# First attention of a four-block kernel: Q projected by halves through K's bank, K through the transposes' bank, a third tile transposed on VectorE, a score ring of 17 places

## What is computed

```python
Q = einsum('bse,hec->bhsc', X, Wq) + bq      # 16 heads, 128 columns: Q1 | Q2, 64 each
K = einsum('bse,hec->bhsc', X, Wk) + bk
V = einsum('bse,hed->bhsd', X, Wv) + bv
A1 = einsum('bhqd,bhkd->bhqk', Q1, K1) * s
A2 = einsum('bhqd,bhkd->bhqk', Q2, K2) * s
P = softmax(A1, axis=-1) - lam * softmax(A2, axis=-1)
O = einsum('bhqk,bhkd->bhqd', P, V)
Y = transpose(O).reshape(...) @ Wo + bo      # then a layer norm
```

## Time and profile before

| | |
|---|---|
| median of 3 runs | 1575.24 us (1575.03 to 1578.04) |
| the profiled execution | 1573.77 us, its span 1572.0 us |
| TensorE matmul busy | 1439.6 us, 92% |
| VectorE busy | 1376.4 us, 88% |
| ScalarE busy | 1198.3 us, 76% |
| GpSimd busy | 1003.8 us, 64% |
| chain that ended last | TensorE 53%, ScalarE 14%, VectorE 13%, issue 11%, GpSimd 7% |
| VectorE, row maxima of the first attention (line 1152) | 512 x 1216 ns = 620.1 us |
| ScalarE, exponentials (line 847) | 512 x 1116 ns = 570.6 us |
| GpSimd, subtractions (line 656) | 256 x 2360 ns = 604.2 us |

### The profile page before, as it was taken

One profiled execution on the slowest core, in us unless ns is written; L12 is line 12 of the kernel. 1 busy time (PEld: TensorE's weight loads), 2 busy tenths in 40 slices (PEclk: granted clock), 3 DMA queues, 4 the chain that ended last, 5 costly groups with the idle time before them and its releaser, 6 DMA issues.

```text
span 1572.0 us, 28031 instructions
## 1 busy us (share of the span) xinstructions
PE 1439.6 (92%) x10243; PEld 588.5 (37%) x10243; DVE 1376.4 (88%) x2107; ACT 1198.3 (76%) x1911; POOL 1003.8 (64%) x727
## 2 busy tenths in 40 slices
PE   5899999999999999999999999986685999999985
PEld 1434443344434443344334433434541222222223
DVE  6798998999899989999999989988687999999947
ACT  4787888888888888888888888874342888888882
POOL 2999998898898988989889889880032011111112
PEclk9999999999999999999999999997696999999997
DMA  4243433343244323433343333420000110000001
GB/s 126 76 105 92 106 86 82 102 112 90 78 103 110 96 77 104 109 92 85 91 107 105 83 91 93 114 68 1 1 22 21 31 35 15 16 16 16 16 16 34
DMA packets 154641, 110.80 MB, mean 70 GB/s; under 512 B 31381, under 2 KB 142906, under 8 KB 154506
## 3 DMA queue, kind: packets, MB, share of 16 engines
q1 hardware_dynamic: 154378, 108.99, 26.5%
q0 software_dynamic: 128, 0.03, 0.0%
HBM read 53.82 MB, written 34.87 MB: 56 GB/s over the span
## 4 chain that ended last, share of the span: by engine, by line
PE 53%; ACT 14%; DVE 13%; issue 11%; POOL 7%; DMA 1%; SPq 0%; POOLq 0%; ACTq 0%; DVEq 0%
PE PS L1573 14%; PE PS L1585 10%; PE PS L1599 9%; ACT ering L847 7%; PE PS L1980 4%; POOL ering L656 3%; DVE nmx L1152 2%; PE PS L1942 2%; DVE region L1172 2%; PE PS L1632 2%; PE PS L1964 2%; ACT region L871 2%; DVE mxp L1479 2%; ACT ering L1059 2%; POOL ering L655 2%
## 5 line engine op out<-in xcount | busy, mean ns | idle before, releaser
L1152 DVE TENSOR_REDUCE nmx<-PS 128x1 f32<-128x1024 f32 x512 | 620.1, 1216 | 54.4 <-PE PS L1574 53.5
L847 ACT ACTIVATE ering<-PS,nmx 128x1024 f32<-128x1024 f32 x512 | 570.6, 1116 | 109.6 <-DVE nmx L1152 109.5
L656 POOL TENSOR_TENSOR ering<-ering 128x1024 f32<-128x1024 f32 x256 | 604.2, 2360 | 21.4
L1573 PE MATMUL PS<-region 64*128 64x512 f16 x1536 | 405.1, 381 | 20.4 <-ACT ering L847 14.5
L1574 PE MATMUL PS<-region 64*128 64x512 f16 x1536 | 405.2, 381 | 0.0
L655 POOL TENSOR_SCALAR ering<-ering,rho 128x1024 f32<-128x1024 f32 x256 | 287.3, 1122 | 95.2 <-DVE rho L1161 94.5
L1479 DVE TENSOR_REDUCE mxp<-PS 128x2 f32<-128x1024 f32 x256 | 304.2, 1222 | 34.3 <-PE PS L1964 29.9
L1059 ACT ACTIVATE ering<-PS 128x1024 f32<-128x1024 f32 x256 | 259.6, 1024 | 70.0 <-PE PS L1942 64.1
L1585 PE MATMUL PS<-ident,ering 128*128 128x128 f32 x1536 | 251.5, 286 | 15.6 <-ACT t L858 8.1
L1585 PEld LDWEIGHTS PS<-ident,ering 128*128 128x128 f32 x1536 | 161.6, 141 | 201.7 <-issue 73.8
L1573 PEld LDWEIGHTS PS<-region 64*128 64x128 f16 x1536 | 112.6, 94 | 261.3 <-ACT ering L847 110.2
(11 more groups left out here) (301 smaller groups left out, 1876.2 us busy)
## 6 DMA issues: line engine op xcount, KB each, us to landing
ptd<-t SPq DMA_DIRECT2D x256, 128.0 KB, 2.4
region<-region SPq DMA_DIRECT2D x64, 256.0 KB, 3.5
t<-ptd SPq DMA_DIRECT2D x44, 256.0 KB, 3.5
region<-ptd SPq DMA_DIRECT2D x44, 256.0 KB, 3.5
va<-ptd SPq DMA_DIRECT2D x20, 256.0 KB, 3.4
acc<-ptd SPq DMA_DIRECT2D x20, 256.0 KB, 3.5
osb<-scr SPq DMA_DIRECT2D x32, 128.0 KB, 3.3
rcp<-scr SPq DMA_DIRECT2D x32, 128.0 KB, 3.3
```

Of the source, the lines that this page charges most:

```text
L656: P.tensor_tensor(e1, e1, e2, ALU.subtract).then_inc(s_sub_ok, 1)
L847: A.activation((E1, E2)[p][s % 4], PS[:, bank:bank + 2, :].rearrange("p a b -> p (a b)"), ACT.Exp, bias=nmx[:, 2 * s + p:2 * s + p + 1], s ...
L1152: V.tensor_reduce(nmx[:, 2 * s + p:2 * s + p + 1], PS[:, bank:bank + 2, :].rearrange("p a b -> p (a b)"), AX.X, ALU.max, negate=True).then ...
L1573: MM(PS[:, bank, :], top[0:64, ql, q], KT[b][0:64, p, kl, :], start=(j == 0), stop=(j == 2))
```

## The change

- `BY_DVE` becomes (0, 1, 2): tile 1 goes over VectorE too. VectorE turns tiles 0, 1, 2 in steps 3, 4, 5, with the two `stage` buffers and DRAM buffers used in turn, counted by c = 3n + i. TensorE turns tiles 3 to 7 (in steps 6, 7, 0, 1, 2).
- Q is projected in two halves of 512 columns in MISC, in steps 0 and 1, where K was; ScalarE and VectorE split each half in steps 1 and 2. Q's place in the ring goes.
- K's halves are projected into TRB, in steps 3 and 5; they are split in steps 3 and 4 (part 0) and 5 (part 1). The first transposes of tile 3 wait for K's last low half, and the first half of K waits for the last eviction of tile 7.
- The ring has 17 places a pass, so it begins on another pair in each pass, and the out-projection's pair moves with it.
- On TensorE, score p=1 stands ahead from step 3 on; the key tiles of values are dealt out as 3, 2, 2, 1; tile 3's two halves stand together behind the values of step 6.
- GpSimd's `part_w` takes Wq and Wk together, three instructions for five, and goes one tile later. SP's load of Wk for the second head moves to the end of its pass.

The diff, cut to its core:

```diff
-        wq_s = sb("wq_s", [128, 128])
-        wk_s = sb("wk_s", [128, 128])
+        wqk_s = sb("wqk_s", [128, 2, 128])
...
-        BY_DVE = (0, 2)
+        BY_DVE = (0, 1, 2)
...
-        def ring(v):
-            at = v + (1 if v >= 1 else 0) + (1 if v >= 5 else 0)
-            return 2 * (at % 3)
-        Y_PAIR, Q_PAIR = 2, 0
+        def turn_of(n, v):
+            return 17 * n + v + (1 if v >= 1 else 0)
+        def ring(n, v):
+            return 2 * (turn_of(n, v) % 3)
+        def y_pair(m):
+            return 2 * ((turn_of(m + 2, 1) - 1) % 3) if m + 2 < last0 else 2
+        def q_done(m, i):
+            return 2 * m + i if m else 1
+        def q_place(m, i):
+            if m == 0:
+                return PS[:, 0:2, :].rearrange("p a b -> p (a b)"), slice(0, T)
+            return MISC, slice(HF * i, HF * i + HF)
+        def k_place(m, part):
+            if m == 0:
+                return (MISC, PS[:, 2, :])[part]
+            return TRB
...
             def store_blocks(n, i):
-                sp.wait_ge(s_bt_ok, 2 * n + i + 1)
-                if n >= 1:
-                    sp.wait_ge(s_ptr_dma[(n - 1) % 2], 64 * ((n - 1) // 2 + 1))
+                c = len(BY_DVE) * n + i
+                sp.wait_ge(s_bt_ok, c + 1)
+                if c >= 2:
+                    sp.wait_ge(s_ptr_dma[c % 2], 32 * (c // 2))
...
-                P.tensor_copy(wqh[:, 0, :], wq_s[:, :])
-                link(P.tensor_copy(wkh[:, 0, :], wk_s[:, :]))
-                P.tensor_tensor(wqh[:, 1, :], wq_s[:, :], wqh[:, 0, :], ALU.subtract)
-                P.tensor_tensor(wkh[:, 1, :], wk_s[:, :], wkh[:, 0, :], ALU.subtract).then_inc(s_wlo_ok, 1)
+                link(P.tensor_copy(wqkh[:, :, 0, :], wqk_s[:, :, :]))
+                P.tensor_tensor(wqkh[:, :, 1, :], wqk_s[:, :, :], wqkh[:, :, 0, :], ALU.subtract).then_inc(s_wlo_ok, 1)
...
                     if s == 2 and nxt and own:
-                        high_k(n + 1, 1)
+                        high_q(n + 1, 1)
...
                     if s == 1 and nxt and own:
-                        high_k(n + 1, 0)
+                        high_q(n + 1, 0)
                     if later and (s + 5) % 8 in BY_PE:
                         keep_t(m, (s + 5) % 8, 0)
                     if own:
                         exponent(n, s, 0)
...
                     if later and (s + 5) % 8 in BY_PE:
                         keep_t(m, (s + 5) % 8, 1)
-                    if s == 2 and nxt and own:
-                        high_q(n + 1)
+                    if s == 5 and nxt and own:
+                        high_k(n + 1, 1)
                     if own:
                         exponent(n, s, 1)
+                    if s == 3 and nxt and own:
+                        high_k(n + 1, 0)
...
                         maximum(n, s, 0)
+                    if s == 4 and nxt and own:
+                        low_k(n + 1, 0)
...
                     if s == 1 and nxt and own:
-                        low_k(n + 1, 0)
+                        low_q(n + 1, 0)
                     if own if s else prv:
                         weigh(n if s else n - 1, (n if s else n - 1) % 2, (s + 7) % 8)
                     if s == 2 and nxt and own:
-                        low_k(n + 1, 1)
+                        low_q(n + 1, 1)
...
-                    if s == 2 and nxt and own:
-                        low_q(n + 1)
-                    if own and s in (3, 5):
-                        turn_blocks(n, s // 2 - 1)
+                    if own and s - 3 in BY_DVE:
+                        turn_blocks(n, BY_DVE.index(s - 3))
+                    if s == 5 and nxt and own:
+                        low_k(n + 1, 1)
...
                 if v == 3 and n >= 2:
                     pe.wait_ge(s_y_ok, n - 1)
-                elif v == 7 and n + 1 < last0:
-                    pe.wait_ge(s_qlo_ok, n + 2)
-                elif v in (1, 2, 5, 6):
+                elif v in (1, 2):
                     at_least(pe, s_exp, u - 1)
                 else:
                     at_least(pe, s_exp, u - 2)
...
                 at_least(pe, s_tr_ev, turned(n, s) + i)
+                if (s, i) == (BY_PE[0], 0) and n + 1 < last0:
+                    pe.wait_ge(s_klo_ok, 2 * (n + 2))
...
-                if m >= 1:
-                    pe.wait_ge(s_exp, 16 * (m - 1) + 3)
-                for i in range(2):
+                if m >= 1 and i == 1:
+                    pe.wait_ge(s_qlo_ok, q_done(m, 0))
+                elif m == 1:
+                    pe.wait_ge(s_klo_ok, 2)
+                    pe.wait_ge(s_xt_ev, 4)
+                elif m >= 2:
+                    pe.wait_ge(s_v_ev, m + 1)
+                    at_least(pe, s_on_ok, m - 2)
+                for k in range(2) if m == 0 else (i,):
...
-                elif part == 1:
+                dst = k_place(m, part)
+                if m >= 1 and part == 1:
                     pe.wait_ge(s_klo_ok, 2 * m + 1)
...
+                elif m >= 1:
+                    at_least(pe, s_tr_ev, turned(m - 1, 0))
...
-            PIECES = {3: (0, 1, 2), 4: (3,), 5: (4, 5, 6), 6: (7,)}
+            PIECES = {3: (0, 1, 2), 4: (3, 4), 5: (5, 6), 6: (7,)}
...
-                    if own and s >= 4:
+                    if s == 5 and nxt and own:
+                        project_k(n + 1, 1)
+                    if own and s >= 3:
                         scores(n, s, 1)
-                    if later and (s + 5) % 8 in BY_PE:
+                    if later and s != 6 and (s + 5) % 8 in BY_PE:
                         turn(m, (s + 5) % 8, 0)
-                    if s == 2 and nxt and own:
-                        project_q(n + 1)
+                    if s == 3 and nxt and own:
+                        project_k(n + 1, 0)
...
                         for j in PIECES[s]:
                             values(n - 1, j)
+                    if s == 6 and later:
+                        turn(m, 3, 0)
...
-                    if own and s < 4:
+                    if own and s < 3:
                         scores(n, s, 1)
                     if later and (s + 5) % 8 in BY_PE:
                         turn(m, (s + 5) % 8, 1)
...
                     if s in (0, 1) and nxt and own:
-                        project_k(n + 1, s)
+                        project_q(n + 1, s)
```

More of the change, by code:

```diff
@@ L147, in two_layers @@
         iota = xs[:, :, :].rearrange("p l t -> p (l t)").bitcast(F32)
-        wqh, wkh = [r16(15360 + 256 * i, 256).rearrange("p (l c) -> p l c", l=2) for i in range(2)]
+        wqkh = r16(15360, 512).rearrange("p (i l c) -> p i l c", i=2, l=2)
+        wqh, wkh = wqkh[:, 0, :, :], wqkh[:, 1, :, :]
         G2 = eflat[:, 4096:8192].rearrange("p (k n) -> p k n", n=N)
@@ L504, in _ @@
                         sp.dma_start(wo_s[64 * k:64 * k + 64, :], a["L0_attn_Wo"][h * D0:h * D0 + D0, :]).then_inc(s_ld_wo, 16)
[L505 to L509, removed]
+                if own and b == 0 and 0 < h < H0 - 1:
+                    sp.wait_ge(s_wlo_ok, h)
                     sp.dma_start(wk_s[:, :], a["L0_attn_Wk"][h + 1]).then_inc(s_ld_wk, 16)
@@ L525, in _ @@
                     load_turned(n, 0)
-                    store_blocks(n, 1)
-                    load_turned(n, 1)
+                    for i in range(1, len(BY_DVE)):
+                        store_blocks(n, i)
+                        load_turned(n, i)
+                if n == 0:
+                    sp.wait_ge(s_k0_mm, 4)
+                    sp.dma_start(wk_s[:, :], a["L0_attn_Wk"][1]).then_inc(s_ld_wk, 16)
             sp.wait_ge(s_wprep_ev, 3)
@@ L838, in exponent @@
                 u = 16 * n + 2 * s + p
-                bank = ring(2 * s + p)
+                bank = ring(n, 2 * s + p)
                 act.wait_ge(s_max, u + 1)
@@ L843, in exponent @@
                     if tile in BY_DVE:
-                        act.wait_ge(s_bt_ok, 2 * prev + BY_DVE.index(tile) + 1)
+                        at_least(act, s_bt_ok, len(BY_DVE) * prev + BY_DVE.index(tile) + 1 if prev >= 0 else 0)
                     else:
@@ L1552, in scores @@
                 u = 16 * n + v
-                bank = ring(v)
+                bank = ring(n, v)
                 if v == 0:
                     pe.wait_ge(s_klo_ok, 2 * (n + 1))
-                    pe.wait_ge(s_qlo_ok, n + 1)
+                    pe.wait_ge(s_qlo_ok, 2 * n + 1)
                     pe.wait_ge(s_qx_dma, 32 * (n + 1))
@@ L1593, in values @@
                 if j == 0:
-                    pe.wait_ge(s_ptr_dma[n % 2], 64 * (n // 2 + 1))
+                    c = len(BY_DVE) * n + len(BY_DVE) - 1
+                    for i in range(2):
+                        pe.wait_ge(s_ptr_dma[i], 32 * ((c - i) // 2 + 1))
                 if j % 4 == 0:
@@ L1612, in to_out, with project_q @@
                     r = slice(64 * half, 64 * half + 64)
-                    mm = MM(PS[:, Y_PAIR + half, :], wo_s[r, :], on[r, :], start=True, stop=True)
```

(3 more changed lines are left out.)

82 lines of the change are left out of this document (38 added, 44 removed).

## The result

| | before | changed |
|---|---|---|
| median | 1575.03 us (7 runs, 1572.80 to 1578.04) | 1582.37 us (7 runs, 1580.47 to 1588.75) |
| span of the profiled execution | 1572.0 us | 1578.7 us |
| VectorE busy | 1376.4 us, 88% | 1412.3 us, 89% |
| TensorE matmul busy | 1439.6 us, 92% | 1402.7 us, 89% |
| ScalarE busy | 1198.3 us, 76% | 1172.0 us, 74% |

The ratio is 1.0051, 95% interval 1.0036 to 1.0066: slower by half a per cent. The time lies inside the range (1566 to 1586), 6.4 us above the 1576.0 forecast, but outside the forecast's own range (1571 to 1580), and its sign is not that of the likeliest case, "same".

What follows compares the result with a forecast made beforehand. A closed chain of hand-overs bounds each pass: 14.06 + 3.37 + 4.44 + 4.24 + 4.86 + 0.86 = 31.83 us against 31.77. With start-up and last pass +0.3 us, 1575.5 on the median's scale, given as 1576.0; range 1566 to 1586.

Steps and rivals of the forecast that it cites:

- the likeliest case, "same": Whole kernel's time unchanged within what a measurement can tell, about 0.2%; chance 0.44, against slower 0.37 and faster 0.19.
- (a): VectorE from max 8 to max 15 (row maxima of scores 8 and 15) without a gap: 14.06 us.
- (b): From max 15 over exponential 15 and score 1 of the next pass to its maximum: 3.37 us.
- (c): VectorE from max 1 to max 3, as before the change: 4.44 us.
- (d): Max 3, exponential 3, high half of Q, then TensorE's stalled second transposes of tile 7: 4.24 us.
- (e): TensorE's score 6, score 7, K half, three key tiles of values, up to score 8: 4.86 us (4.71 to 4.98).
- (f): From the start of score 8 on TensorE to its maximum on VectorE: 0.86 us.
- closed chain: One steady pass as hand-overs between engines, from max 8 to the next max 8: 31.83 us, against 31.77 before.
- the second path: From max 8 over low K and TensorE's tiles 3 to 5 to score 1: 16.62 us against 16.57, no slack.
- the slower rival: TensorE's second path is longer by x, each pass growing by x; 0.23 us gives 1582; chance 0.30.
- Passes 0 to 3 are held by GpSimd's side work, which stays: Start-up: GpSimd releases tile 5 of pass 3 at 164.06 as before, putting max 8 of pass 4 at 179.9.
- The faster rivals: VectorE's own 29.98 us plus a hand-over, 1555 us, chance 0.12; TensorE alone, 1542 us, chance 0.03.

Runs made afterwards that it cites:

- h1: `e1` with only half of tile 1's transposes done on VectorE, behind max 9; ratio 0.9946 to the kernel before, median 1566.49 us.
- e1: Changed kernel with the second head's Wk loaded early, at the start of pass 0, into a free buffer; ratio 1.0024 to the kernel before, median 1578.02 us.
- b1: Kernel before with only the late load of the second head's Wk, at the end of SP's pass 0; ratio 1.0074, span 1585.5 us.
- c1: Changed kernel with VectorE's wait for GpSimd's last subtraction moved ahead of the 16 one-hot rows; ratio 1.0039 to the kernel before.
- h0: `e1` with only half of tile 0's transposes done on VectorE, ahead of max 8; ratio 1.0008 to the kernel before, median 1575.39 us.
- f1: Changed kernel with GpSimd's iota moved behind its last subtraction and VectorE's wait for it behind the one-hot rows; ratio 1.0034 to the kernel before.
- g3: `e1` with tile 7's first eviction and exp 4 ahead of high Q, score 14 between tile 3's transposes, max 5 ahead of low Q; ratio 0.9969, 1570.10 us.
- g4: `g3` with the move of GpSimd's iota and of VectorE's wait for it, as in `f1`; ratio 0.9963 to the kernel before, median 1569.12 us.
- b2: `b1` with VectorE's weights of rows (two comparisons, a sum, a reciprocal) moved from pass 1 to pass 4; ratio 1.0065, span 1583.3 us.

## Why the prediction was right and wrong

- **The pass, 31.83: right, 31.84**, by pieces (max 8 at 503.00 to max 8 at 534.84): (a) 14.03 for 14.06; (b) 3.59 for 3.37; (c) 4.45 for 4.44; (d) 4.16 for 4.24; (e) 4.75 for 4.86; (f) 0.86 for 0.86. The mechanism, a closed chain with idle time ahead of max 8, holds; that the sum is right to 0.01 is luck, since (b) is 0.22 over and the others together 0.21 under.
- **(b) was too short by 0.22, and part of it is the second path.** Exp 15 starts 1.32 after max 15 (1.25), and score 1 at 519.76, 0.15 later than exp 15 and a hand-over allow (518.35 + 1.26 = 519.61). Counted from max 8, the second path took 16.76 us for 16.62. The chain of waits runs through this path:

```profile
511.59 0.43 PE PS L1626 x2
512.02 0.07 issue
512.10 0.64 PE PS L1610 x4
...
512.76 0.61 ACT va L878
...
518.16 1.08 PE PS L1640 x4
```

  Tile 4 to tile 5 is 3.77, for 3.59: the out-projection starts 0.78 behind score 0 (517.33 to 518.11), and tile 5's group 1.06 after it. So the slower rival is there as a mechanism, with x = 0.15, and "no slack" was right; what it took, (d) and (e) gave back. That the median fell on this rival's number, 1582, is a coincidence: its 6 us were to lie in the passes, which cost 2.00. `h1` shows its price when the first path is shortened: 0.23 of 0.53.
- **(e): K ahead of the values costs 0.67**, the low end of 0.68 to 0.86. The Trainium skill, "TensorE: Matmul & The Clock Gate", Part 3, lets a weight load overlap only on other row groups, which would have made it the upper end; here as between scores, the trace doesn't show that. (The same part, in "The mechanism", also allows a load into the background weight buffer, which the prediction left out; with it the page doesn't contradict the 0.67.)
- **"Passes 0 to 3 are held by GpSimd's side work, which stays" was the step that failed.** The prediction priced GpSimd's small instructions and where they stand, and the third tile's DMAs in SyncE's queue, but not the load of Wk, which the diff moves behind them. It put max 8 of pass 4 at 179.9; it is at 184.62, 4.7 later, and the 4.89 of the profiled pair is 73% of the span's difference. `e1` and `b1` show the late load as a cause; of its size the medians give 4.4 (1582.37 less 1578.02), the profiled pair's pass 4 only 1.6. With the load early, pass 4 is still 3.30 us later in `e1` than before, of which 3.00 are GpSimd's two waits for VectorE; what else of the change brings these on was not tested.
- **The last pass** was right to 0.2: 30.06 from max 8 to max 8 (1012.49 to 1042.55) for 29.86, then 12.72 for 12.74.
- **Behind the last maximum nothing was priced.** The sum ended at the last maximum and took the rest of the kernel as it was; the one-hot rows add 1.46. VectorE now reaches them earlier relative to GpSimd: its subtractions go on for 4.79 us beside them, before for 3.05. Three rows stand beside subtractions, and `c1` shows that without them none is long.
- **Values never waited for a DMA**, as priced, though stores land in 2.9 us on the profile's page, for 2.4.
- **The faster rivals** had VectorE at its own sum or TensorE alone as the bound. `h0` refutes the first (0.00 for 0.53 us of VectorE's work), the pass itself the second: TensorE's busy time fell from 31.10 to 29.91, and the pass grew from 31.77 to 31.84.

What stays open: the start-up differs between executions of the same code, so no split of one profiled pair is exact. The adding of Y in pass 4 started at 171.55, 172.49 and 177.84 in three kernels that are alike up to there (changed, `c1`, `f1`), and at 167.96 and 171.26 in two others (`g3`, `g4`); in `f1` the two comparisons took 2.41 us and GpSimd waited 2.93 and 1.61 in pass 1. Why a delay of 1.5 to 2.6 us on VectorE grows to 4.5 to 5.7 us of GpSimd's waits was not taken apart. The stretch from the last adding of Y to the end, which no experiment touched, also took from 492.5 (`g3`, `g4`) to 495.5 us (before, changed).

## What to carry to other kernels

When a change moves a load, read the queue that it is moved into as an engine of its own: list what stands ahead of it, and who stands still for it; here the start-up, with one load at the wrong end of a queue, cost more (4.89 us in the profiled pair) than the 27 passes, the last pass and the end together (1.78). In a closed chain of hand-overs an engine's busy share doesn't tell what its work is worth; leaving out half of an instruction at one place and then at another tells it. And a step taken out of the chain shows only the next one: shortening by 0.57 gave 0.14, and the rest came in part when the new last one, exp 4, was moved too.

## What the runs showed of the hardware

An fp32 comparison of 128 x 256 on VectorE, from SBUF to SBUF, takes 0.34 us alone and up to 2.5 us when GpSimd subtracts; the 512 row maxima out of PSUM keep their 1.2 us (1.183 to 1.244) in passes full of the same subtractions. Waiting for GpSimd (`c1`) shows that it is the neighbour and not the rows: all 16 at 0.344 to 0.353 us. The Trainium skill, "SBUF — State Buffer", section "Who interferes with whom", says that VectorE's two-port modes and GpSimd hold one pair of ports in turn, each for a whole instruction; the longest row, 2.51 us, against the 2.35 us subtraction beside it (1061.93 to 1064.28), agrees; in which mode the comparisons ran, no row tells. The iota, which only writes, held one up for 1.97 us (`f1`).

How long the two comparisons in pass 1 take depends on what GpSimd does beside them: 0.70 us (before), 0.95 (changed), 2.41 (`f1`) and 3.30 (`b1`). In `b1` the first stands beside a subtraction's first instruction and the second beside its other (97.71 to 100.07); before, they run across the gap between two subtractions (87.99 to 88.31). That the long ones set off GpSimd's later waits is shown for `b1` alone, by `b2`; with short ones, `g3` still had waits of 0.84 and 1.67 us in pass 3.
